# Attention layer: the two halves of a row-maximum block one behind the other, and one VectorE pass over both

## The chip, the core and the metric

The kernel runs on one core of a Trainium2 chip. The metric is device time in microseconds of one launch. Three runs of the kernel before took 2716.44, 2714.80 and 2719.52 us; the median is 2716.44.

## The reference

Two layers over a batch of 8 images of 512 channels and 32x32 places (N = 1024). The first is group norm, attention over the places with 8 heads of 64, a projection and a residual; all in float32:

```
h = group_norm(x, w, b)
q, k, v = split(qkv_w @ h + qkv_b)          # 8 heads of 64 each
attn = softmax(q^T k * 64 ** -0.5)          # 1024 x 1024 for each head
x = x + proj_w @ (v attn^T) + proj_b
```

The second layer picks 256 places of each image, attends among them and projects. The change doesn't touch its arithmetic.

## The kernel before

Float32 products are made of three float32r products of high and low parts (ScalarE makes the high part, VectorE the low one by a subtraction). The first layer is `attention_layer`; each engine has one program written out in order, and semaphores count what is done.

**Steps.** For each of 64 heads (8 images of 8 heads) there are 8 steps, so 512 steps. One step handles one tile t of scores, 1024 columns: two key tiles of 128 for one half (512) of the queries. TensorE in a step (`step`, line 478): the low product of tile t-2 (`weigh_low`, 2 matmuls, line 474), the scores of tile t (4 matmuls of 512 columns, lines 447 and 451) into one of two ring buffers in PSUM, the first half of a row-maximum block (line 428), the projection part that is due in the step, the high product of tile t-1 (`weigh_high`, 4 matmuls), the second half of the block. ScalarE takes two exponentials of the tile (lines 544 and 546): one rounded to float32r, one kept in full. VectorE's `p_low` subtracts them (line 695). The score buffer of tile t-2 and the low product both wait for `p_low` of t-2.

**Row maxima.** Softmax needs the maximum of each query's scores before they are exponentiated. A block is 128 queries against all 1024 keys, taken with high parts alone: two matmuls of 512 columns whose weights are every fourth column of q. There are 8 blocks for a head, one in each step, three steps ahead of their use (`max_tile`). Each half lies in a PSUM bank of its own and is reduced by VectorE on its own (line 679) into `row_max`; after four blocks a small maximum of the two halves (`top_of_halves`, line 687) gives `row_max_top`, and SyncE copies it into a row of `q_low_max` (`max_to_row`).

**Projections.** A unit is 12 matmuls of 512 columns in one PSUM bank: k, q or v of the pair of heads that comes next, or one part of the output (o) of the image before. `PAIR_STEPS` says at which step a unit begins, and whether it is taken whole or in two halves of 6 matmuls in neighbouring steps. "g" is a small matmul for the group norm of the next image, "vt" four 128x128 transposes of v. A finished unit is read by ScalarE (`kq_high`, line 575, `v_full`, `v_high`) and by VectorE (`kq_low`, line 708, `v_low`, `residual`). In the same way VectorE has, at set steps, the statistics of the next image's tiles (`tile_stats`, in the fourth head of an image), the low part of its normed form (`normed_low`, sixth and seventh head) and the low part of the output (`o_low`, first step of every second head). GpSimd multiplies by the reciprocals (line 878).

**Banks.** Scores take two ring buffers of two banks, the weighted sums one bank. Three banks (`BANKS`) serve both units and halves of blocks. `bank_events` lists in order of the program what needs a bank, in units of one matmul, and `assign_banks` gives each the bank that is expected to be read soonest; `READ_BEHIND` says how long behind its last matmul each kind is expected to be read. A first half may not take the bank of a unit that ended in the step before. `fill_free` makes TensorE wait, before the first matmul into a bank, until what was there has been read. VectorE's order in a step (line 799): second half of the block of the step before, the maximum of halves where it is due, `p_low` of the tile before, first half of this step's block, then the low parts of the units that ended in the step before, then statistics and the rest.

Of the kernel before, what the change touches and what calls it, by code (L numbers as in the profile page):

```python
# [14 lines left out]
P = 128  # L15
# [127 lines left out]
READ_BEHIND = dict(m=8, k=26, q=26, v=12, vt=28, o=26, g=22)  # L143


def bank_events():
# [4 lines left out]
    def take(e, closed=None):  # L151
        if e not in last:
            events.append((e, closed))
        last[e] = at
# [4 lines left out]
    for h in range(ALL_HEADS):  # L159
        for s in range(STEPS):  # L160
            block = max_tile(h, s)
            at += 7
            if block:

                take(("m", *block, 0), before(h, s))
# [3 lines left out]
            at += 5  # L169
            if block:  # L170
                take(("m", *block, 1))
# [6 lines left out]
def assign_banks():  # L178
# [3 lines left out]
    for e, closed in events:  # L182
        open_banks = [i for i in range(BANKS) if closed is None or holder[i] not in UNITS.get(closed, [])]
# [29 lines left out]
def attention_layer(nc, x, w_pieces, bias_half, bias_v, bias_o, gn_wb, x1, consts):  # L213
# [23 lines left out]
    sb("spare", [P, 2, N])  # L237
# [5 lines left out]
    mcol = sb("row_max", [P, 2, 2, NT])  # L243
# [14 lines left out]
    ring, pv = tiles[:, 0:2, :], tiles[:, 2, HALF:N]  # L258
    banks = [tiles[:, 2, 0:HALF], tiles[:, 3, 0:HALF], tiles[:, 3, HALF:N]]
# [11 lines left out]
    s_mtop = sem("s_mtop")  # L271
# [36 lines left out]
    def max_bank(h, i, n):  # L308
        return banks[BANK["m", h, i, n]]
# [17 lines left out]
    def tensor(pe, then):  # L327
        mm = nc.tensor.matmul

        def max_count(h, i, n):  # L330
            return (h * NT + i) * 2 + n + 1

        def fill_free(u):
# [3 lines left out]
            if w[0] == "m":  # L337
                pe.wait_ge(s_mx, max_count(*w[1:]))
# [66 lines left out]
        def take_first_max(i, n):  # L405

            if n == 0 and i % 4 == 0:
# [3 lines left out]
            m = i * 2 + n  # L411
            if m > 3:
                pe.wait_ge(s_mx, m - 3)
            first = (i // 4) * HALF + i % 4
            mm(ring[:, i % 2, n * HALF:(n + 1) * HALF], q1[:, 0, first:first + HALF - 3:4],
               k1[:, 0, n * HALF:(n + 1) * HALF], start=True, stop=True).then_inc(s_max, 1)

        def take_max(h, i, n):

            g = h // 2  # L420
            if h % 2 == 0 and i == 0:
                pe.wait_ge(s_kql, kq(("k", g, n)))
# [5 lines left out]
            mm(max_bank(h, i, n)[:, :], q1[:, q_slot(h), first:first + HALF - 3:4], k1[:, k_slot(h), n * HALF:(n + 1) * HALF],  # L428
               start=True, stop=True).then_inc(s_max, 1)

        def scores(h, s):
            t, wk, wq = h * STEPS + s, k_slot(h), q_slot(h)
            if t > 1:
                pe.wait_ge(s_pl, t - 1)
            else:
                pe.wait_ge(s_mx, 2 * (NT - AHEAD))
# [41 lines left out]
        def step(h, s):  # L478
# [5 lines left out]
            if block:  # L484
                take_max(*block, 0)
# [1569 lines left out]
```

## Time and profile before

| what | value |
|---|---|
| median of 3 runs | 2716.44 us |
| span of the one profiled execution | 2718.4 us |
| TensorE matmul | 2619.7 us busy (96%), 11856 matmuls |
| TensorE weight loads | 2181.7 us (80%) |
| VectorE | 2055.1 us (76%) |
| ScalarE | 1578.5 us (58%) |
| GpSimd | 221.9 us (8%) |

The span is the profiled execution's time from its first to its last instruction; no other time of that execution is known. Matmuls overlap, so that a busy TensorE isn't TensorE at its peak: a matmul of 512 columns is shown with some 0.39 us and the next starts 0.23 us after it. The first layer lasts until about 2217 us, the second from there on.

### The profile page before, as it was taken

The numbers are of one execution on the slowest core, as the hardware profiler recorded it, in microseconds if no ns is written. First come the engines' busy times: TensorE is split into PE (matmuls) and PEld (weight loads), VectorE is DVE, ScalarE is ACT, GpSimd is POOL, SyncE is SP. The second block draws the span as 40 slices with busy tenths as digits, with TensorE's granted clock in tenths as the row PEclk, the third lists the DMA queues.
The fourth block names the chain that finished last, engine by engine and source line by source line (L and its number), as shares of the span: only waits on it lengthen the run. The fifth ranks groups of instructions, "written<-read, shape, count | busy, mean of one in ns | idle before, by whom it ended". The sixth has DMA issues, their size and how long they took to land.

```text
span 2718.4 us, 33180 instructions
## 1 busy us (share of the span) xinstructions
PE 2619.7 (96%) x11856; PEld 2181.7 (80%) x11856; DVE 2055.1 (76%) x3294; ACT 1578.5 (58%) x1930; POOL 221.9 (8%) x134
## 2 busy tenths in 40 slices
PE   6999999999999999999999999999999987899998
PEld 5788888888888888888888888888888876688887
DVE  6788768876887688768876887688767867878864
ACT  4667646764676467646764676567646663334311
POOL 1000000000000000000000000000000012111010
PEclk9999999999999999999999999999999999899999
DMA  4512232223222322232223222321322335466444
GB/s 156 177 50 80 67 103 61 79 71 100 64 78 67 101 67 76 63 107 67 65 72 109 66 59 79 109 67 48 90 83 58 112 127 203 171 215 246 165 164 170
DMA packets 154849, 279.48 MB, mean 103 GB/s; under 512 B 51776, under 2 KB 52032, under 8 KB 154176
## 3 DMA queue, kind: packets, MB, share of 16 engines
q1 hardware_dynamic: 152128, 268.98, 31.4%
q0 software_dynamic: 2560, 8.39, 1.0%
q8 instruction: 96, 1.57, 0.2%
q14 instruction: 65, 0.53, 0.1%
HBM read 180.04 MB, written 63.18 MB: 89 GB/s over the span
## 4 chain that ended last, share of the span: by engine, by line
PE 83%; DVE 9%; issue 3%; DMA 2%; ACT 1%; SPq 0%; POOL 0%; POOLq 0%; DVEq 0%; ACTq 0%
PE tiles L372 9%; PE tiles L373 8%; PE tiles L374 8%; PE tiles L474 8%; PE tiles L451 8%; PE tiles L428 8%; PE tiles L468 8%; PE tiles L467 8%; PE tiles L447 7%; PE tiles L1321 5%; PE tiles L1371 2%; DVE row_max L679 2%; DVE p_low L695 2%; DVE h_low L787 1%; PE tiles L383 1%
## 5 line engine op out<-in xcount | busy, mean ns | idle before, releaser
L679 DVE TENSOR_REDUCE row_max<-tiles 128x1 f32<-128x512 f32 x1014 | 694.5, 685 | 443.4 <-PE tiles L428 440.6
L544 ACT ACTIVATE p_high<-tiles 128x1024 fp32r<-128x1024 f32 x512 | 525.5, 1026 | 595.8 <-PE tiles L451 595.1
L695 DVE TENSOR_TENSOR p_low<-tiles,p_high 128x1024 fp32r<-128x1024 f32 x512 | 623.0, 1217 | 7.0 <-ACT tiles L546 6.2
L546 ACT ACTIVATE tiles<-tiles 128x1024 f32<-128x1024 f32 x512 | 523.0, 1021 | 0.0
L467 PE MATMUL tiles<-p_high,v_high 128*128 128x512 f32 x1024 | 406.5, 397 | 2.2 <-ACT num_den L562 1.5
L428 PE MATMUL tiles<-k_high_low,q_high_high 128*128 128x512 f32 x1014 | 404.8, 399 | 0.2 <-DVE row_max L679 0.2
L468 PE MATMUL tiles<-p_high,v_low 128*128 128x512 f32 x1024 | 402.0, 393 | 0.0
L428 PEld LDWEIGHTS tiles<-k_high_low,q_high_high 128*128 128x128 f32 x1014 | 312.5, 308 | 48.6 <-DVE row_max L679 5.7
L474 PE MATMUL tiles<-p_low,v_high 128*128 128x512 f32 x1024 | 325.8, 400 | 14.9 <-DVE p_low L695 14.6
L451 PE MATMUL tiles<-q_low_max,k_high_one 65*128 65x512 f32 x1024 | 325.8, 399 | 1.9 <-DMA q_low_max<-row_max_top 1.8
L372 PE MATMUL tiles<-h_high,w_high 128*128 128x512 f32 x768 | 304.6, 397 | 17.3 <-DVE row_max L679 8.3
L878 POOL TENSOR_TENSOR o_normed<-num_den,o_normed 64x1024 f32<-64x1024 f32 x64 | 153.5, 2399 | 2046.1 <-DMA o_normed<-rec_rows 2046.1
L447 PE MATMUL tiles<-q_high_high,k_high_low 128*128 128x512 f32 x1024 | 316.8, 391 | 0.0
L373 PE MATMUL tiles<-h_low,w_high 128*128 128x512 f32 x768 | 301.7, 393 | 0.0
L374 PE MATMUL tiles<-h_high,w_low 128*128 128x512 f32 x768 | 300.4, 391 | 0.0
L447 PEld LDWEIGHTS tiles<-q_high_high,k_high_low 128*128 128x128 f32 x1024 | 192.0, 188 | 47.6
L451 PEld LDWEIGHTS tiles<-q_low_max,k_high_one 65*128 65x128 f32 x1024 | 193.2, 189 | 45.6 <-DMA q_low_max<-row_max_top 4.4
L474 PEld LDWEIGHTS tiles<-p_low,v_high 128*128 128x128 f32 x1024 | 189.7, 188 | 44.9 <-DVE p_low L695 25.2
L467 PEld LDWEIGHTS tiles<-p_high,v_high 128*128 128x128 f32 x1024 | 192.5, 188 | 38.8 <-ACT num_den L562 2.3
L468 PEld LDWEIGHTS tiles<-p_high,v_low 128*128 128x128 f32 x1024 | 192.6, 188 | 38.0
L372 PEld LDWEIGHTS tiles<-h_high,w_high 128*128 128x128 f32 x768 | 145.8, 190 | 43.9 <-issue 24.2
L374 PEld LDWEIGHTS tiles<-h_high,w_low 128*128 128x128 f32 x768 | 145.1, 189 | 32.4
(167 smaller groups left out, 3138.1 us busy)
## 6 DMA issues: line engine op xcount, KB each, us to landing
x_tiles<-in_x SPq DMA_DIRECT2D x64, 512.0 KB, 5.4
w_high<-w_split SPq DMA_DIRECT2D x126, 256.0 KB, 2.8
w_low<-w_split SPq DMA_DIRECT2D x126, 256.0 KB, 3.0
k_high_one<-k_high_low SPq DMA_DIRECT2D x128, 128.0 KB, 2.3
q_high_high<-q_high_high SPq DMA_DIRECT2D x128, 128.0 KB, 2.3
o_normed<-rec_rows SPq DMA_DIRECT2D x64, 256.0 KB, 3.7
x<-x_tiles SPq DMA_DIRECT2D x32, 512.0 KB, 4.0
x_full<-x SPq DMA_DIRECT2D x32, 512.0 KB, 8.3
```

The source lines that it names most:

```text
L372: mm(fill[:, :], w1, high[:, c, cols], start=(c == 0), stop=False)
L374: last = mm(fill[:, :], w2, high[:, c, cols], start=False, stop=(c == CT - 1))
L428: mm(max_bank(h, i, n)[:, :], q1[:, q_slot(h), first:first + HALF - 3:4], k1[:, k_slot(h), n * HALF:(n + 1) * HALF], start=True, stop=True ...
L447: mm(out[:, n * HALF:(n + 1) * HALF], k1[:, wk, keys[n]], q1[:, wq, queries], start=True, stop=False)
L451: last = mm(out[:, n * HALF:(n + 1) * HALF], k2[0:HD + 1, wk, keys[n]], q2[0:HD + 1, wq, queries], start=False, stop=True)
L467: mm(pv[:, :], weights_of(v1, t, n), p, start=(t % 4 == 0 and n == 0), stop=False)
L468: last = mm(pv[:, :], weights_of(v2, t, n), p, start=False, stop=False)
L474: last = mm(pv[:, :], weights_of(v1, t, n), pl[:, t % 2, n * HALF:(n + 1) * HALF], start=False, stop=(t % 4 == 3 and n == 1))
L544: nc.scalar.activation(ph[:, r, :], ring[:, r, :], ACT.Exp, scale=ATT_SCALE).then_inc(s_ph, 1)
L546: nc.scalar.activation(ring[:, r, :], ring[:, r, :], ACT.Exp, scale=ATT_SCALE).then_inc(s_p32, 1)
L679: nc.vector.reduce_max(mcol[:, h % 2, n, i:i + 1], max_bank(h, i, n)[:, :], AX_X).then_inc(s_mx, 1)
L695: tt(pl[:, r, :], ring[:, r, :], ph[:, r, :].bitcast(F32), ALU.subtract).then_inc(s_pl, 1)
```

## The change

- Both halves of a block are multiplied one behind the other. Where only one unit has a part in the step, they go behind that part; where two have (a unit and a transpose of v), ahead of them (`pair_first`).
- The second half always has the bank in the middle (`MIDDLE`), the first one of the outer banks; units have the outer ones alone. The banks are laid out side by side, so that one VectorE pass of 1024 columns reads both; the weighted sums move to the bank in front of them. A bank is open only when its holder's last matmul is behind.
- One maximum for each block goes straight into `row_max_top`; `row_max`, `top_of_halves` and its semaphore are gone. SyncE's copy waits for the fourth block's maximum.
- VectorE's order in a step: the low parts of the units that ended in the step before, the maximum of this step's block, `p_low` of this step's own tile, then the rest.
- The opening's blocks are handled the same way over the ring buffers.

```diff
-READ_BEHIND = dict(m=8, k=26, q=26, v=12, vt=28, o=26, g=22)
+READ_BEHIND = dict(m=9, k=26, q=26, v=12, vt=28, o=26, g=22)
+MIDDLE = 1
+def pair_first(h, s):
+    spans = (before(h, s), (h, s))
+    begun = {u for at in spans for u, parts in PARTS.get(at, []) if u[0] not in ("g", "vt")}
+    here = {u for u, _ in PARTS.get((h, s), [])}
+    going = {u for u in begun if u in here}
+    return len(going | here) > 1
...
-            at += 7
-            if block:
-                take(("m", *block, 0), before(h, s))
+            at += 6
+            if block and pair_first(h, s):
+                at += 1
+                for n in range(2):
+                    take(("m", *block, n))
             for u, parts in PARTS.get((h, s), []):
                 at += {"g": 1, "vt": 2}.get(u[0], 6 * len(parts))
                 take(u)
-            at += 5
-            if block:
-                take(("m", *block, 1))
+            if block and not pair_first(h, s):
+                at += 1
+                for n in range(2):
+                    take(("m", *block, n), UNITS.get((h, s), []))
+            at += 4
...
-    for e, closed in events:
-        open_banks = [i for i in range(BANKS) if closed is None or holder[i] not in UNITS.get(closed, [])]
+    for e, closed, at in events:
+        among = (MIDDLE,) if e[0] == "m" and e[-1] == 1 else (0, 2)
+        open_banks = [i for i in among if holder[i] not in closed and (holder[i] is None or end[holder[i]] <= at)]
...
-    ring, pv = tiles[:, 0:2, :], tiles[:, 2, HALF:N]
-    banks = [tiles[:, 2, 0:HALF], tiles[:, 3, 0:HALF], tiles[:, 3, HALF:N]]
+    ring, pv = tiles[:, 0:2, :], tiles[:, 2, 0:HALF]
+    pool_row = tiles[:, 2:4, :].rearrange("p a n -> p (a n)")[:, HALF:(1 + BANKS) * HALF]
+    banks = [pool_row[:, i * HALF:(i + 1) * HALF] for i in range(BANKS)]
...
-            fill_free(("m", h, i, n))
+            for n in range(2):
+                fill_free(("m", h, i, n))
...
             scores(h, s)
-            if block:
-                take_max(*block, 0)
+            if block and pair_first(h, s):
+                take_max(*block)
             for u, parts in PARTS.get((h, s), []):
                 unit_work(u, parts)
+            if block and not pair_first(h, s):
+                take_max(*block)
             if t > 0:
                 weigh_high(t - 1)
-            if block:
-                take_max(*block, 1)
...
+        def reduce_max(h, i):
+            if h > 1 and i % 4 == 0:
+                dve.wait_ge(s_mrow[i // 4], 16 * (h - 1))
+            dve.wait_ge(s_max, h * NT + i + 1)
+            first = min(max_banks(h, i))
+            nc.vector.reduce_max(mtop[:, h % 2, i:i + 1], pool_row[:, first * HALF:(first + 2) * HALF], AX_X
+                                 ).then_inc(s_mx, 1)
...
             if t > 0:
-                behind = before(h, s)
-                done = max_tile(*behind)
-                if done:
-                    reduce_max(*done, 1)
-                    if done[1] % 4 == 3:
-                        top_of_halves(done[0], done[1] // 4)
-                p_low(t - 1)
+                for u in UNITS.get(before(h, s), []):
+                    unit_low(u)
             if block:
-                reduce_max(*block, 0)
-            if t > 0:
-                for u in UNITS.get(behind, []):
-                    unit_low(u)
+                reduce_max(*block)
+            p_low(t)
...
         def max_to_row(h, i):
-            sp.wait_ge(s_mtop, 2 * h + i + 1)
+            sp.wait_ge(s_mx, h * NT + 4 * i + 4)
```

## Rows read from the trace of the kernel before

**Rows 1.** The page's chain that ended last, shares of the span by engine.
```profile
PE 83%; DVE 9%; issue 3%; DMA 2%; ACT 1%; SPq 0%; POOL 0%; POOLq 0%; DVEq 0%; ACTq 0%
```

**Rows 2.** Stretches: us; busy (instructions) PE, PEld, DVE, ACT, POOL; PE clock; DMA share; GB/s.
```profile
582.60:856.70 274.10, 271.85 (x1190) 226.13 (x1188) 209.79 (x297) 175.76 (x205) 20.18 (x9) 1.00 0.27 78
2217.00:2718.00 501.00, 453.99 (x2427) 385.18 (x2425) 367.45 (x905) 160.34 (x274) 55.49 (x51) 0.97 0.55 197
46.00:57.00 11.00, 9.02 (x28) 6.67 (x29) 3.13 (x5) 4.25 (x7) 0.00 (x0) 0.69 0.11 39
57.00:110.00 53.00, 49.12 (x212) 39.81 (x211) 43.31 (x62) 36.86 (x49) 0.00 (x0) 1.00 0.65 209
```

**Rows 3.** Groups (busy, mean ns, idle before); then merged time line of the opening.
```profile
L679 DVE TENSOR_REDUCE row_max<-tiles 128x1 f32<-128x512 f32 x1014 | 694.5, 685 | 443.4 <-PE tiles L428 440.6
...
L687 DVE TENSOR_TENSOR row_max_top<-row_max 128x4 fp32r<-128x4 f32 x128 | 37.6, 294 | 4.4
...
37.68 1.01 PEld L415 LDWEIGHTS tiles<-k_high_low,q_high_high 128*128 128x128 f32 x4
...
38.34 3.68 DVE L669 TENSOR_REDUCE row_max<-tiles 128x1 f32<-128x512 f32 x6 [1.17 <-PE tiles L415]
```

**Rows 4.** Time line, one step: start, us, engine, line, operation, output, inputs, count.
```profile
804.60 0.62 PE L447 MATMUL tiles<-q_high_high,k_high_low 128*128 128x512 f32 x2
...
805.14 1.23 DVE L695 TENSOR_TENSOR p_low<-tiles,p_high 128x1024 fp32r<-128x1024 f32 x1
...
806.28 0.68 DVE L679 TENSOR_REDUCE row_max<-tiles 128x1 f32<-128x512 f32 x1
...
806.66 1.02 ACT L546 ACTIVATE tiles<-tiles 128x1024 f32<-128x1024 f32 x1
...
807.60 1.36 ACT L575 ACTIVATE k_high_low<-tiles,bias_qk 64x512 fp32r<-64x512 f32 x2
...
808.05 0.39 PE L428 MATMUL tiles<-k_high_low,q_high_high 128*128 128x512 f32 x1
...
808.48 0.69 DVE L679 TENSOR_REDUCE row_max<-tiles 128x1 f32<-128x512 f32 x1 [0.40 <-PE tiles L428]
```

**Rows 5.** Time line, TensorE: first score matmuls of steps 3.0, 3.1, 4.2-4.4, 6.0-6.2.
```profile
697.31 0.40 PE L447 MATMUL tiles<-q_high_high,k_high_low 128*128 128x512 f32 x1
...
702.65 0.62 PE L447 MATMUL tiles<-q_high_high,k_high_low 128*128 128x512 f32 x2
...
738.16 0.62 PE L447 MATMUL tiles<-q_high_high,k_high_low 128*128 128x512 f32 x2
...
741.29 0.39 PE L447 MATMUL tiles<-q_high_high,k_high_low 128*128 128x512 f32 x1
...
745.80 0.39 PE L447 MATMUL tiles<-q_high_high,k_high_low 128*128 128x512 f32 x1
...
793.11 0.39 PE L447 MATMUL tiles<-q_high_high,k_high_low 128*128 128x512 f32 x1
...
796.99 0.40 PE L447 MATMUL tiles<-q_high_high,k_high_low 128*128 128x512 f32 x1
...
800.46 0.62 PE L447 MATMUL tiles<-q_high_high,k_high_low 128*128 128x512 f32 x2
```

**Rows 6.** Time line about step 2.7: a GpSimd product and the maximum of halves.
```profile
693.14 2.39 POOL L878 TENSOR_TENSOR o_normed<-num_den,o_normed 64x1024 f32<-64x1024 f32 x1 [36.60 <-DMA o_normed<-rec_rows]
...
694.51 1.04 DVE L687 TENSOR_TENSOR row_max_top<-row_max 128x4 fp32r<-128x4 f32 x1
```

**Rows 7.** Time line, VectorE: the low part of one k unit, two heads.
```profile
740.34 1.51 DVE L708 SCALAR_TENSOR_TENSOR k_high_low<-tiles,bias_qk,k_high_low 64x512 fp32r<-64x512 f32 x2
```

**Rows 8.** Time line, end of step 2.7: a residual and the load behind it.
```profile
695.47 1.21 DVE L695 TENSOR_TENSOR p_low<-tiles,p_high 128x1024 fp32r<-128x1024 f32 x1
...
696.74 0.30 PEld L474 LDWEIGHTS tiles<-p_low,v_high 128*128 128x128 f32 x2 [0.51 <-DVE p_low L695]
```

**Rows 9.** Time line, VectorE: statistics of one x tile.
```profile
713.22 1.28 DVE L780 BATCH_NORM_STATS2 bn_parts<-x_tiles 128x6 f32<-128x512 f32 x2
```

More of the change, by code:

```diff
@@ L235, in attention_layer @@
     pl = sb("p_low", [P, 2, N], F32R)
-    sb("spare", [P, 2, N])
+    sb("spare2", [P, 4, HALF])
     nd = sb("num_den", [P, 2, N])
@@ L242, in attention_layer @@
     v32 = sb("v_full", [P, HALF])
-    mcol = sb("row_max", [P, 2, 2, NT])
+    sb("spare", [P, 2, 2, NT])
     mtop = sb("row_max_top", [P, 2, NT], F32R)
@@ L306, in fill_of, with max_banks @@
         return banks[BANK[u]]
-    def max_bank(h, i, n):
-        return banks[BANK["m", h, i, n]]
+    def max_banks(h, i):
+        return [BANK["m", h, i, n] for n in range(2)]
     h32 = Count([(0, 0)] + [(b, t) for b in range(1, BATCH) for t in range(CT)])
@@ L403, in unit_work, with take_first_max @@
                 project(u, parts)
[L405 to L407 removed]
+        def take_first_max(i):
+            if i % 4 == 0:
                 pe.wait_ge(s_kqh, kq(("q", 0, i // 4)))
@@ L425, in take_max @@
                 pe.wait_ge(s_twin["q", i // 4], 32 * (g + 1))
-            fill_free(("m", h, i, n))
+            for n in range(2):
+                fill_free(("m", h, i, n))
             first = (i // 4) * HALF + i % 4
-            mm(max_bank(h, i, n)[:, :], q1[:, q_slot(h), first:first + HALF - 3:4], k1[:, k_slot(h), n * HALF:(n + 1) * HALF],
-               start=True, stop=True).then_inc(s_max, 1)
+            to = max_banks(h, i)
+            for n in range(2):
+                last = mm(banks[to[n]], q1[:, q_slot(h), first:first + HALF - 3:4],
+                          k1[:, k_slot(h), n * HALF:(n + 1) * HALF], start=True, stop=True)
+            last.then_inc(s_max, 1)
         def scores(h, s):
@@ L497, in tensor @@
                 for i in range(4):
-                    for n in range(2):
-                        take_first_max(i, n)
+                    take_first_max(i)
             if u == ("v", 0, 1):
-                for n in range(2):
-                    take_first_max(4, n)
+                take_first_max(4)
         pe.wait_ge(s_pset, 3)
@@ L852, in vector @@
         for i in range(4):
-            for n in range(2):
-                reduce_first_max(i, n)
-        top_of_halves(0, 0)
-        for n in range(2):
-            reduce_first_max(4, n)
+            reduce_first_max(i)
+        reduce_first_max(4)
         for u in PROLOGUE[6:]:
@@ L864, in vector @@
                 step(h, s)
-        p_low(TILES - 1)
         reciprocal(ALL_HEADS - 1)
```

48 lines of the change are left out of this document (18 added, 30 removed).

## The prediction

> **What bounds the kernel now.** I read the chain of waits first: TensorE holds 83% of the chain that ended last, VectorE 9% [rows 1]. The stretch table comes next. It has to be read by stage: one whole batch image of the first layer (a "batch" below) lasts 274.10 us and TensorE is busy 271.85 of them at full clock; the second layer, from about 2217 us, lasts 501 us and is not touched by the change beyond one wait at its start [rows 2]. So in the part that changes TensorE is the bound, there is next to nothing to win on VectorE as such (209.79 busy of 274.10 [rows 2]), and only two things count: the holes in TensorE's stream that go, and those that come. The third view is the time line of one half-unit step, scores to scores 4.15 us [rows 4], and the fourth the starts of steps that last longer than their matmuls need [rows 5].
>
> Holes of one batch now, from [rows 5] (heads 0 to 7, steps 0 to 7, so 3.0 is head 3 step 0): 3.0 lasts 702.65 - 697.31 = 5.34 where 4.15 do: 1.19; 4.3 4.51: 0.36; 4.2 3.13 where 12 matmuls and the small sum need 2.94: 0.19; the same two again at 4.5 and 4.6: 0.55; 6.0 3.88 and 6.1 3.47 where 2.79 do (twelve matmuls): 1.09 and 0.68. Step 2.7 loses 0.3 on average: there the tiny maximum of halves took 1.04 instead of 0.16 us, until GpSimd's product was over (693.14 + 2.39), and the residual pass behind it came late [rows 6]. Together about 4.3 us a batch. The whole of what can be won is six to eight times that, some 30 us, and a few us at the start, where TensorE is idle 1.98 + 3.88 us up to 110 us [rows 2].
>
> **The change part by part.** Matmuls: the same 1014, same strided weights. Two back to back follow each other at the pace of the rest: six maxima of the opening over two ring buffers keep VectorE fed at 0.61 us each (3.68 for six), and their loads, 0.31 long, start 0.23 apart (four in 1.01) [rows 3]. I take 0 (bounds -2 to +4 us in all).
>
> VectorE: a 128x512 maximum has 685 ns, a start-to-start pace of 0.61 [rows 3]; a 128x1024 pass over PSUM 1.23 us, the next one starting 1.14 after it (805.14 to 806.28 [rows 4]). The fused maximum isn't in the trace. Bounds: 0.61 (no dearer than one half) and 1.37 (twice 685 ns). I take 1.13, the row of the same width and memory, a hundredth off for its own variation. So a block costs 1.13 in place of 1.22, and the 128 maxima of halves (294 ns each, 37.6 us [rows 3]) go. In themselves both are worth nothing, TensorE's stream covers them; what they free is the 0.3 at step 2.7. The VectorE page of the Trainium skill ("VectorE: DVE Perf Modes", The perf-mode tier table) says that a reduction runs at single rate from any memory and gives (N+151)/0.96 ns for one fp32 pass: 1.22 us at 1024, 0.69 at 512. By it the lower bound is out; the trace shows this for 512 (685 ns) only.
>
> Order: VectorE did, in a step, second half of the block before, residual of the tile before, first half, low part of a finished projection. Now: low part of the projection that ended a step ago, then the fused maximum, then the residual of this step's own tile. The residual comes earlier for who needs it: it ends 5.3 us after the scores' start and is wanted at about 7.6. Its holes at 6.0/6.1 stay, those at 2.7 and 3.0 shrink. Copying to the row needs no step of its own and SyncE's DMA leaves some 0.9 us sooner; nothing waits for it in the steady state.
>
> Banks: this is where it costs. Three banks, but now the second half of every block has the middle one, so projections and first halves share two. A unit that runs in step t+1 holds one; the pair of step t+1 therefore must take the one whose projection ended in step t, unless that has been read. Following the planner's rule, k and q are handed over like this at 2.3, 2.5, 3.2, 5.0, 5.2, 6.4, 6.6, 7.0, 7.2 with half a unit in front, at 4.2 and 4.5 with only the group sum in front. When is the bank read? Clock the step from its first score matmul (804.60 [rows 4]). Scores end at 0.93, six projection matmuls start from 0.93 to 2.06, the pair at 2.29 and 2.53, v matmuls to 3.67, the low part to 4.15. VectorE starts 0.43 after the last matmul (808.05 to 808.48), so the maximum at 2.96, the residual at 4.09 (its input, the second exponential, ends at 3.08: 806.66 + 1.02), the low part of k or q at 5.22, and that takes 1.51 [rows 7]: 6.73. ScalarE's half of it (807.60, 1.36 long) is ready at 4.4 and not in the way. Into the next step that is 6.73 - 4.15 = 2.58, its weight load can go at 2.64 (0.06 from VectorE's end to the load, 696.68 to 696.74 [rows 8]), and it was due at 2.06 (a load is 0.23 ahead of its matmul): 0.58 late. A load that comes late gives 0.12 back (scores at 697.31 are 0.57 behind the late load where three spacings of 0.23 are usual [rows 5, 8]). Stall 0.46. The next step starts with the same phases, so stalls don't grow or melt.
>
> The list for a batch, by the same phases:
> - eight plain hand-overs (all above but 3.2): 8 x 0.46 = 3.7
> - 3.2: the statistics of an x tile (1.28 for both halves [rows 9], 1.44 with the small aggregate) stand ahead of q's low part in step 3.1; load at 4.08 for 2.06: 1.9
> - 4.2 and 4.5: the pair is due right behind the small sum, load at 0.81, bank free 2.64: 2 x 1.7 = 3.4
> - 3.4 (pair first, then a transpose into its bank): the maximum waits for statistics and reciprocal of step 3.3, ends 3.85, the transposes were due at 2.54: 1.25. The like of it at 0.3, 5.4, 7.4 without statistics: 3 x 0.2 = 0.6
> - 1.1, behind o_low and q's low part: 0.2; 3.0: 0.2; 6.0 and 6.1, where a residual of h stands in each step as before: 0.45 + 0.6 = 1.05
>
> Sum 12.3 against 4.3: +8.0 a batch, six full batches +48. The first batch has the later heads' list (+6.5 over its own holes) and an opening where whole projections wait for a maximum that now goes behind them: I take -5 of the 5.9 us idle there [rows 2] (it can't be more than 5.9, nor above 0), +1.5 net. The last batch has no statistics, sums or h: about 3.1 against 4.7, and 1 less in its last steps: -2.6. Sum +47. The one profiled execution lasts 2718.4, 2.0 over the median 2716.4 of the runs (0.07%, inside their spread), so 2716.4 + 47 = 2763.
>
> What waits behind the new wait: TensorE is in order, so v matmuls of the tile before, the low part and the next scores all stand behind the pair; ScalarE and VectorE then idle, both have room (175.76 and 209.79 of 274.10 [rows 2]). Before, the pair's second half came last in the step, 1.6 us later, and any of three banks could serve.
>
> **Rivals.**
> (a) Faster: the hand-over is met. It decides at the fused maximum's pace: at 0.61 instead of 1.13 (the lower bound) k's low part ends at 6.2, load 2.11 for 2.06, and the eight plain stalls are gone; 3.2 keeps 1.4, 4.2 and 4.5 1.2 each, the rest 0.3, so 4.1 a batch against 4.3, -1 for six; the opening -5, the rest of the first batch -1.4, the last -5.4: 2704. For it: nothing but that the trace has no such pass. Against: both widths cost by the element [rows 3, 4].
> (b) Dearer: the pass takes two halves' full 1.37. Each of some 18 hand-overs is 0.24 later: +4.3 a batch, +31 in all: 2794. For it: it spans two banks. Against: 1.23 for a residual over two banks [rows 4].
> (c) Phases 0.25 sooner than I stack them (they are sums of five small gaps): 12 binding places, -3 a batch and a little in the outer ones, -23: 2740.
> (d) The change doesn't do what it says: the planner finds banks that were read anyway and moves holes about, no net: 2716. Against: two banks for two takers.
>
> **How the numbers follow.** Forecast 0.70, (a) 0.09, (b) 0.09, (c) 0.08, (d) 0.04. Predicted 2763. The range 2728 to 2790 holds the forecast with the small bounds (2750 to 2778, its own range) and (c) and reaches near (b); (a), (d) and part of (b) are left out. Changes under 0.2% (5.4 us) can't be told from none here. Faster by more than that 0.10 ((a) and a little), within it 0.05, slower 0.85.
>
> **What would show it.** Right: the pair's weight loads wait for the low part of k or q, for some 3.7 + 1.9 + 3.4 = 9 us a batch, steps 4.2 and 4.5 last about 4.6 instead of 3.1, 3.2 about 6 instead of 4.15, steps with an output projection stay at 5.51; the fused maximum has about 1.22 us; matmul count unchanged; second layer within 1 us. Wrong: a fused maximum near 0.7 us (then (a)), or steps 2.3, 5.2, 6.4 still at 4.15 with 1.22 (then my phases or my reading of the banks), or new waits on the residual p_low, which I say has more than 0.1 us to spare everywhere, 6.0 and 6.1 the tightest.

## The result: 3.8% slower, and where the 106 us stand

Over four runs each the changed kernel takes 2824.48 us (2815.54 to 2826.21) and the kernel before 2717.98 us: a ratio of 1.0379, 95% interval [1.036, 1.0399]. That is 106.5 us more, outside the range; 46.6 were forecast. The profiled spans are 2718.4 and 2821.7 us, 103.3 apart, and these 103.3 are accounted for below.

The page of the changed kernel first: the chain that ended last, then groups (busy us, mean ns of one | idle before and what ended it).

```profile
PE 70%; DVE 17%; issue 7%; DMA 3%; ACT 2%; SPq 1%; POOL 0%; POOLq 0%; DVEq 0%; ACTq 0%
...
L699 DVE TENSOR_REDUCE row_max_top<-tiles 128x1 fp32r<-128x1024 f32 x507 | 619.8, 1222 | 652.7 <-PE tiles L448 652.1
...
L448 PE MATMUL tiles<-k_high_low,q_high_high 128*128 128x512 f32 x1014 | 349.4, 426 | 57.6 <-DVE k_high_low L720 32.0
L448 PEld LDWEIGHTS tiles<-k_high_low,q_high_high 128*128 128x128 f32 x1014 | 275.6, 313 | 112.4 <-DVE k_high_low L720 46.2
```

VectorE had 9% of the chain [rows 1] and has 17%, although it works less: its one maximum of 1222 ns replaces two of 685 [rows 3]. The pair's weight loads, L448, now stand idle for 112.4 us. The waits of the weight loads say for whom (what waited, for which line; us in all, times, longest):

```profile
PEld tiles L448 <- DVE k_high_low L720: 46.2, 44, 1.7
PEld tiles L448 <- DVE q_low_max L720: 33.7, 38, 2.0
PEld tiles L388 <- issue: 23.5, 19, 6.9
PEld tiles L399 <- DVE row_max_top L699: 19.2, 31, 1.4
...
PEld tiles L472 <- DMA q_low_max<-row_max_top: 13.3, 13, 2.8
```

L720 is the low part of a finished k or q: the bank's last reader. L399 is the transpose of v, which takes the bank of the pair just ahead. L388 is the first matmul of a projection; its "issue" holds a wait that the profile has no releaser for, of which more at step 1.1.

Step by step, from the start of one step's first score matmul to the next one's, for one image; each value is the median over images 1 to 6 (the images are numbered 0 to 7). "More, all" is the sum over the steps named in the row, and "forecast" what the prediction's list comes to for them:

```
steps                                   before       changed      more, all    forecast
2.3 2.5 6.6 | 6.4 (after k)             4.15         4.86 | 5.02   3.00        1.84
5.0 7.0 | 5.2 7.2 (after q)             4.15         4.79 | 4.73   2.44        1.84
3.2                                     4.15         6.11          1.97        1.9
4.2 4.5, and 4.3 4.6 behind them        3.13, 4.51   4.85, 4.17    2.76        2.3
3.4                                     4.61         5.77          1.16        1.25
0.3 5.4 7.4                             4.61         4.8           0.49        0.6
1.1                                     5.51         7.09          1.58        0.2
2.7 3.0                                 3.07, 5.34   2.76, 4.56   -1.09       -1.3
6.0 6.1                                 3.89, 3.46   3.48, 3.40   -0.47       -0.7
other steps with 12 projection matmuls  5.51         5.54          0.37        0
steps with a transpose alone            3.22         3.31          0.36        0
```

The rows sum to 12.6 us an image, against 7.9 forecast. With the steps that moved by a hundredth or two it is 12.9, or 13.1 if each step's difference is taken image by image before the median. The images themselves, 0 to 7, take 14.4, 16.7, 15.4, 14.1, 12.8, 13.1, 12.8 and 0.5 us more; with 1.75 ahead of the first scores and 1.87 behind the last image's they make the 103.3 (the rest is rounding).

How one hand-over looks: TensorE's pair waits in step 2.3 of image 2 (start, us, engine, line, operation). The step begins at 712.39.

```profile
711.20 1.22 DVE L699 TENSOR_REDUCE row_max_top<-tiles 128x1 fp32r<-128x1024 f32 x1 [1.80 <-PE tiles L448]
...
712.34 1.22 DVE L707 TENSOR_TENSOR p_low<-tiles,p_high 128x1024 fp32r<-128x1024 f32 x1
712.39 0.62 PE L468 MATMUL tiles<-q_high_high,k_high_low 128*128 128x512 f32 x2
...
713.59 1.51 DVE L720 SCALAR_TENSOR_TENSOR k_high_low<-tiles,bias_qk,k_high_low 64x512 fp32r<-64x512 f32 x2
...
714.47 0.40 PE L390 MATMUL tiles<-h_high,w_low 128*128 128x512 f32 x1
...
715.15 0.55 PEld L448 LDWEIGHTS tiles<-k_high_low,q_high_high 128*128 128x128 f32 x2 [0.73 <-DVE k_high_low L720]
...
715.62 0.19 PEld L488 LDWEIGHTS tiles<-p_high,v_high 128*128 128x128 f32 x1
```

Maximum, residual and low part follow each other without a gap. The low part ends at 715.10, 2.71 into the step; the pair's load goes at 2.76, where it was due at 2.08, with the last projection matmul (714.47). The order of VectorE's three passes makes the stall: the residual p_low stands between the maximum and the low part that TensorE waits for.

### The profile page after: what moved, and what is told of

Read it like the earlier page. It is cut to its first block, busy times and chain, and to the rows that moved or that the text cites. A ratio compares the mean times of both kernels' runs of the same rounds, so it can differ in the third digit from the quotient of the medians.

```text
span 2821.7 us, 32922 instructions
## 1 busy us (share of the span) xinstructions
PE 2665.3 (94%) x11856; PEld 2188.6 (78%) x11856; DVE 1979.7 (70%) x2654; ACT 1579.2 (56%) x1930; POOL 221.9 (8%) x134
## 4 chain that ended last, share of the span: by engine, by line
PE 70%; DVE 17%; issue 7%; DMA 3%; ACT 2%; SPq 1%; POOL 0%; POOLq 0%; DVEq 0%; ACTq 0%
PE tiles L448 9%; PE tiles L388 7%; PE tiles L390 7%; PE tiles L389 7%; PE tiles L472 6%; PE tiles L489 6%; PE tiles L495 6%; PE tiles L488 6%; PE tiles L468 6%; DVE p_low L707 5%; PE tiles L1323 5%; DVE k_high_low L720 2%; PE tiles L1373 2%; DVE q_low_max L720 2%; DVE row_max_top L699 2%
## 5 line engine op out<-in xcount | busy, mean ns | idle before, releaser
L699 DVE TENSOR_REDUCE row_max_top<-tiles 128x1 fp32r<-128x1024 f32 x507 | 619.8, 1222 | 652.7 <-PE tiles L448 652.1
L448 PE MATMUL tiles<-k_high_low,q_high_high 128*128 128x512 f32 x1014 | 349.4, 426 | 57.6 <-DVE k_high_low L720 32.0
L448 PEld LDWEIGHTS tiles<-k_high_low,q_high_high 128*128 128x128 f32 x1014 | 275.6, 313 | 112.4 <-DVE k_high_low L720 46.2
L495 PE MATMUL tiles<-p_low,v_high 128*128 128x512 f32 x1024 | 319.3, 393 | 1.8 <-DVE p_low L707 1.8
L388 PE MATMUL tiles<-h_high,w_high 128*128 128x512 f32 x768 | 302.6, 394 | 8.7 <-DVE h_low L799 6.8
L472 PEld LDWEIGHTS tiles<-q_low_max,k_high_one 65*128 65x128 f32 x1024 | 192.9, 189 | 53.3 <-DMA q_low_max<-row_max_top 13.3
L388 PEld LDWEIGHTS tiles<-h_high,w_high 128*128 128x128 f32 x768 | 145.5, 189 | 44.5 <-issue 11.4
L389 PEld LDWEIGHTS tiles<-h_low,w_high 128*128 128x128 f32 x768 | 145.7, 190 | 35.4
```

Of the source, the lines that this page charges most:

```text
L388: mm(fill[:, :], w1, high[:, c, cols], start=(c == 0), stop=False)
L389: mm(fill[:, :], w1, low[:, c, cols], start=False, stop=False)
L448: last = mm(banks[to[n]], q1[:, q_slot(h), first:first + HALF - 3:4], k1[:, k_slot(h), n * HALF:(n + 1) * HALF], start=True, stop=True)
L472: last = mm(out[:, n * HALF:(n + 1) * HALF], k2[0:HD + 1, wk, keys[n]], q2[0:HD + 1, wq, queries], start=False, stop=True)
L495: last = mm(pv[:, :], weights_of(v1, t, n), pl[:, t % 2, n * HALF:(n + 1) * HALF], start=False, stop=(t % 4 == 3 and n == 1))
L699: nc.vector.reduce_max(mtop[:, h % 2, i:i + 1], pool_row[:, first * HALF:(first + 2) * HALF], AX_X).then_inc(s_mx, 1)
```

## The experiments

Theory: every microsecond lost is in VectorE's *order*. Projections and first halves share two banks, and a bank's last reader comes late since other passes stand ahead of it; o_low, which the output projection needs, was pushed back in the same way. Main rival: VectorE's *amount* of work, or the fused pass itself. All ratios are against the kernel before, run on the same chip. Steps that another effect touches, a lower clock of TensorE behind a stall, are named where it matters; the section on the prediction comes back to it.

**o_first.** One line moved: o_low from behind p_low to ahead of the maximum.

```
+            if h % 2 == 1 and h > 1 and s == 0:
+                o_low(h // 2 - 1)
             if block:
                 reduce_max(*block)
             p_low(t)
...
-            if h % 2 == 1 and h > 1 and s == 0:
-                o_low(h // 2 - 1)
```

> The changed kernel with one move: o_low (the low part of the finished output pair) goes ahead of the step's fused maximum on VectorE, not behind the residual p_low. Theory A: the 1.58 us that step 1.1 lost (7.09 for 5.54) is TensorE's output projection waiting for o_low, which the change pushed from about 2.9 to about 6.6 us into step 1.0. Then 1.1 returns to 5.54 in seven images, -11 us, about 2813. Rival: it waits for the projection weights, whose transfers were issued at 659.1 and 659.7 in the same step; then nothing moves, 2824.

2812.94 us, 1.0346 [1.0328, 1.0363]; span 2811.7. Step 1.1 went from 7.09 to 5.54 in every image that has it, and no other step's median moved by more than 0.03 but that of 4.2. That one is 4.83 to 4.85 in four of the images 0 to 6 and 6.30, 5.75 and 5.61 in the other three, where the granted clock was 0.73 to 0.85. The changed kernel's rows show the mechanism (step 1.1 of image 2 begins at 658.20):

```profile
658.15 1.22 DVE L707 TENSOR_TENSOR p_low<-tiles,p_high 128x1024 fp32r<-128x1024 f32 x1
...
659.29 1.22 DVE L804 TENSOR_TENSOR o_low<-o_normed,o_high 128x1024 fp32r<-128x1024 f32 x1
...
660.57 0.19 PEld L388 LDWEIGHTS tiles<-o_high,w_high 128*128 128x128 f32 x1 [1.73 <-issue]
```

The first load of the output projection comes 0.06 behind the end of o_low (660.51). In o_first o_low starts at 654.74 and the projection finds it done. The profile names no releaser ("issue") there: an idle stretch without a name is still a wait, and the semaphores in the code say for what.

**low_first.** The low part of a projection right behind the maximum of the step that ends it, ahead of p_low:

```
-            if t > 0:
-                for u in UNITS.get(before(h, s), []):
-                    unit_low(u)
             if block:
                 reduce_max(*block)
+            for u in UNITS.get((h, s), []):
+                unit_low(u)
             p_low(t)
```

> The changed kernel with VectorE's order changed: the low parts of the units that end in step t are taken right behind that step's fused maximum and ahead of its p_low, not a step later. Theory A (loop): a hand-over step is set by the loop pair, maximum 1.14, p_low 1.14, low part 1.51, bank free, pair, 4.8 us against a step of 4.16; taking p_low out of the loop brings 2.3, 2.5, 5.2, 6.6, 7.2 and 5.0, 6.4, 7.0 back to 4.16 (-5.4 an image), 3.2 too (-1.9, the statistics come behind), 4.2 and 4.5 from 4.85 to about 4.05 (-1.6); in return the residual of 2.6 comes late for step 3.0 (+0.8). Net -8 an image, -57 in all, about 2767. Rival B: the stalls come from matmuls and the fused pass meeting in neighbouring banks, whatever the order; then the same steps keep 4.7 to 4.9 and the time 2824 within 5. Rival C: p_low, now a low part later, is the next thing late in every k and q step, 2824 or more.

2775.96 us, 1.0211 [1.0191, 1.0232]; span 2775.3: 46 less than the changed kernel in the spans, where 57 were expected. All nine hand-overs, 2.3 to 7.2, are back at 4.16 us, 3.2 among them; 3.0 too; 4.2 and 4.5 are at 3.86. So the hand-over is the main loss, and it is one of order. It is given back in part at 1.1, where o_low now stands behind still more: 8.6 us instead of 7.09 in images 3 and 6, and 10.2 or more in the other five, where the granted clock was 0.83 and less. The order alone costs 1.5 there and the clock as much again; the expectation had neither. More is given back at 2.7 (3.62) and 6.0 (3.81), where p_low is late for its own reader: 13.8 us of waits for it in place of 3.7.

```profile
PEld tiles L388 <- issue: 31.7, 11, 6.9
PEld tiles L399 <- DVE row_max_top L699: 19.2, 31, 1.4
PEld tiles L495 <- DVE p_low L707: 13.8, 15, 1.4
```

**extras_first.** VectorE's other passes (o_low, statistics of the x tiles but that of 3.4, the small scalings, low parts of the next input and of fresh weights) ahead of the maximum; units and p_low stay.

```
+            if b < BATCH:
+                if h % HEADS == 3 and s in (1, 3, 5):
+                    tile_stats(b, (1, 3, 4, 5).index(s))
...
+            if h % 2 == 1 and h > 1 and s == 0:
+                o_low(h // 2 - 1)
+            if t > 0 and t - 1 + EARLY < len(FRESH):
+                split_low(t - 1 + EARLY)
             if block:
                 reduce_max(*block)
             p_low(t)
```

> The changed kernel with VectorE's occasional work (x statistics of steps 3.1, 3.3 and 3.5, group scale, low parts of h and o, the weight splits of the opening) moved from behind p_low to ahead of the step's fused maximum, where VectorE sits idle 1.7 us. Theory A: 1.1 -1.58, 3.2 from 6.11 to about 4.85 (-1.3), 3.4 from 5.77 to about 4.8 (-1.0), nothing at 6.0 and 6.1, -4 us an image from the second on and a few us in the opening, whose weight splits no longer hold up SyncE's queue: -28 to -35 in all, about 2792. Rival: the maximum comes later by what was put ahead of it, so nothing is won, 2820 to 2830.

2787.76 us, 1.0249 [1.023, 1.0268]; span 2793.6. 1.1 is at 5.54, 3.2 at 4.73, 3.4 at 4.75; the plain hand-overs are untouched, as they should be. What stands ahead of the pair's last reader costs in full, one pass ahead of the maximum nearly nothing.

**halves.** The changed order and banks, but two maxima of 128x512 and the small maximum over four blocks, as before:

```
-            nc.vector.reduce_max(mtop[:, h % 2, i:i + 1], pool_row[:, first * HALF:(first + 2) * HALF], AX_X)
+            nc.vector.reduce_max(mcol[:, h % 2, 0, i:i + 1], banks[to[0]], AX_X)
+            nc.vector.reduce_max(mcol[:, h % 2, 1, i:i + 1], banks[to[1]], AX_X)
+            if i % 4 == 3:
...
+                tt(mtop[:, h % 2, blocks], mcol[:, h % 2, 0, blocks], mcol[:, h % 2, 1, blocks], ALU.max
```

> The changed kernel with the fused pass alone undone: the same banks, order and pairs of matmuls, but two 512-wide maxima back to back and the small maximum of halves after four blocks. Theory A: the pass is worth 0.06 us a step (0.60 + 0.60 against 1.14) plus the small maximum; it binds in some 19 steps an image: +8 to +15 us, 2832 to 2839. Rival B (the pass over two banks is what is slow): 15 us or more faster, below 2810.

2847.77 us, 1.0472 [1.0455, 1.049]. The fused pass by itself is a gain, some 23 us in this kernel, more than the 8 to 15 that were expected of it. It isn't what made the change slow.

**both.** low_first and extras_first together.

> VectorE's order: o_low, the statistics of the x tiles (but that of step 3.4), the small scalings, the low parts of the next image's input and of the fresh weights ahead of the fused maximum; the low part of a projection right behind the maximum of its own step, ahead of the residual p_low. If all that is lost is lost in VectorE's order (my theory), the two gains add: low_first's +7.5 us an image less 4.7 at step 1.1 (10.21 to 5.54, o_low no longer behind anything) less 1.0 at 3.4 gives about +1.9 an image, some +10 in the first image and the opening: about 2738 (2732 to 2746). If the later low part only trades places with the others (rival: VectorE's sum of work in a step is the bound, whatever the order), the extras push the maximum back and it stays at 2765 to 2775.

2736.99 us, 1.0055 [1.004, 1.0071]; span 2734.9. 87 of the 103 us are gone with not one instruction less and the same banks. So VectorE's order made most of the loss, and the rival, that the amount of work binds, falls.

**best.** both, and on TensorE the pair behind the weighing in steps with a group sum, the transpose of v behind it in steps where the pair comes first; on VectorE a unit that ends ahead of an empty step is read in that step.

```
+def behind(h, s):
+    kinds = {u[0] for u, _ in PARTS.get((h, s), [])}
+    return "vt" in kinds if pair_first(h, s) else "g" in kinds
...
             if t > 0:
                 weigh_high(t - 1)
+            for u, parts in behind_it:
+                unit_work(u, parts)
+            if block and not pair_first(h, s) and late:
+                take_max(*block)
```

> As both, and three places moved on top: in steps 4.2 and 4.5 the pair goes behind the weighing with p_high, in steps 0.3, 3.4, 5.4 and 7.4 the transpose of v does, and a unit that ends ahead of a step without a projection has its low part taken in that step, ahead of the maximum. By my theory each of the waits left in low_first goes: 0.7 each at 4.2 and 4.5, 0.14 each at 0.3, 3.4, 5.4, 7.4, 0.86 at 2.7, 0.3 at 6.0: 3.1 us an image or 22 in all, about 2717, no difference from the kernel before. If the banks bind by themselves (rival: two banks for projections and first halves can't be filled without a stall, whatever the order), about 2735 as both.

2725.55 us, 1.0018 [1.0009, 1.0027]; 8 us short of the expectation. 2.7 is back at 2.76 and the transposes' steps at 4.58, but 3.0 pays 0.39 for the first (its scores wait for the copy of the maxima, 1.0 us in image 2), 4.2 and 4.5 gained 0.25 each instead of 0.7 (the residual takes the place of the pair's wait), and 3.6 lost 0.92. The last is plain in VectorE's rows of best: two statistics in a row between two maxima, and in step 3.6 (from 999.38) a transpose that waits for the second maximum.

```profile
997.32 1.28 DVE L807 BATCH_NORM_STATS2 bn_parts<-x_tiles 128x6 f32<-128x512 f32 x2
...
998.95 1.29 DVE L807 BATCH_NORM_STATS2 bn_parts<-x_tiles 128x6 f32<-128x512 f32 x2
...
1000.40 1.17 DVE L714 TENSOR_REDUCE row_max_top<-tiles 128x1 fp32r<-128x1024 f32 x1
```

```profile
1001.62 0.66 PE L406 MATMUL tiles<-identity,v_full 128*128 128x128 f32 x4 [1.16 <-DVE row_max_top L714]
```

**best2.** Each statistic alone behind p_low, where VectorE has no low part of a unit; the low part of a fresh weight between maximum and p_low; low parts of the input in 6.0 and 6.1 behind p_low.

```
+STATS_AT = [(3, 2), (3, 3), (3, 5), (4, 0)]
...
             if block:
                 reduce_max(*block)
+            if t > 0 and t - 1 + EARLY < len(FRESH):
+                split_low(t - 1 + EARLY)
...
             p_low(t)
+            if (h % HEADS, s) in STATS_AT:
+                tile_stats(b, STATS_AT.index((h % HEADS, s)))
```

> The kernel best, where step 3.6 still lost 1.49 us an image (4.71 for 3.22 before) because VectorE made two x tiles' statistics in a row between two maxima (997.3 to 1000.4 of its trace). Here each statistic stands alone behind p_low, in steps 3.2, 3.3, 3.5 and 4.0, in which VectorE has no low part of a projection; the low parts of the next input in 6.0 and 6.1 go behind p_low again; and the low part of a fresh weight goes behind the maximum and ahead of p_low. Theory (TensorE loses only where its bank is read late): 3.6 back to 3.31, 6.0 to 3.5, the first image 1 to 3 us shorter: 1.5 an image, 2712 (2706 to 2718), about 0.3% under the kernel before. Rival (VectorE's work of heads 3 and 4 is too much wherever it stands): the loss moves to 4.1 and 4.2, 2722 to 2727.

2707.25 us, 0.9959 [0.9944, 0.9975]: 0.41% faster than the kernel before and 117 us faster than the changed one. 3.6 is at 3.33 us, 6.1 at 2.76, and the first image is 4.7 us shorter than in best. How much of this is the change's own can't be read from it: some of the moves (the input's low parts in 6.0 and 6.1, where 6.1 took 3.46 in the kernel before; the statistics; the low parts of fresh weights) might serve the kernel before as well, and it was not run with them. Chain and the pair's own row:

```profile
PE 80%; DVE 10%; ACT 4%; issue 3%; DMA 2%; SPq 1%; POOL 0%; DVEq 0%; POOLq 0%; ACTq 0%
...
L457 PE MATMUL tiles<-k_high_low,q_high_high 128*128 128x512 f32 x1014 | 327.4, 404 | 5.9 <-DVE row_max_top L716 5.8
```

The idle time ahead of the pair's matmuls is down from 57.6 to 5.9 us.

**best2_halves.** best2 with the fused pass undone in the same way as in halves.

> best2 with the fused pass undone: two maxima of 128x512 for each pair and the small maximum over four blocks, all else the same. It asks what the one pass over both banks is worth in an order that suits it. Theory: its gain is 0.08 us in each step and the small maximum, and pays only where a bank is waited for; with most of these waits gone it is worth less than the 23 us it was worth in the changed kernel: 2715 to 2722. Rival: VectorE's time is what binds, and it is worth 20 us or more again: 2732 or over.

2726.44 us, 1.0031 [1.0019, 1.0043]: 19.2 us over best2, above the theory's 2715 to 2722 and under the rival's 2732. So the fused pass keeps its value in a good order. The steps that differ are few: 3.0 (+1.02), 2.7 (+0.33), 6.0 (+0.33), 3.4 (+0.13), 4.0 (+0.12). In images 1 and 6, 3.0 lasts 7.1 instead of 5.6, at a lower granted clock: some 3 us of the 20.3 between the two spans are that. In 3.0 of image 2 (from 700.18), for one, a projection's first matmul waits for the second maximum of the pair before it, and VectorE's passes stand back to back:

```profile
697.54 0.80 DVE L726 TENSOR_TENSOR row_max_top<-row_max 128x4 fp32r<-128x4 f32 x1
698.27 1.21 DVE L734 TENSOR_TENSOR p_low<-tiles,p_high 128x1024 fp32r<-128x1024 f32 x1
699.40 1.50 DVE L747 SCALAR_TENSOR_TENSOR q_low_max<-tiles,bias_qk,q_high_high 64x512 fp32r<-64x512 f32 x2
...
701.54 0.68 DVE L722 TENSOR_REDUCE row_max<-tiles 128x1 f32<-128x512 f32 x1
```

```profile
702.37 0.47 PE L398 MATMUL tiles<-h_high,w_high 128*128 128x512 f32 x1 [0.79 <-DVE row_max L722]
```

Here the small maximum, 0.80 instead of 0.16 us, pushes four passes back, as in the kernel before [rows 6]. With it gone they are on time.

**plain_weights.** The changed kernel; the pair's weights are 128 neighbouring columns instead of every fourth. The maxima then belong to other queries, so this is a probe and no kernel to use.

```
-                last = mm(banks[to[n]], q1[:, q_slot(h), first:first + HALF - 3:4],
+                last = mm(banks[to[n]], q1[:, q_slot(h), i * P:(i + 1) * P],
```

> The changed kernel, where the pair takes 128 neighbouring columns of q as its weights in place of every fourth one (the maxima then belong to other queries, so the output is another one); everything else is as it was. If the long weight loads of the pair (0.31 us in place of 0.19) add to a hand-over that stalls (theory), each of the nine hand-overs loses about 0.12 less and steps with an output projection 0.03: 1.5 us an image, about 2812. If loads are hidden even there (rival), the same time within 2 us, 2824.

2804.29 us, 1.0304 [1.029, 1.0318]; span 2810.7. The stalled hand-overs are 0.08 to 0.12 shorter (2.3 at 4.75), the transposes' steps 0.11 to 0.13, those with an output projection 0.04, as the theory has it. It all comes to more than the 12 us expected, since most of the other steps are 0.01 to 0.05 shorter too: the medians of all steps but 4.2, 4.3 and 4.5 sum to 2.7 us less an image, some 19 in seven images, and the two times differ by 20.2. The spans differ by 11.0 only: the profiled execution is the slowest of the five (2812.59), and in it 4.2, 4.3 and 4.5 are 2.5 us an image longer, with a granted clock under 1 in five of the images 1 to 6. The sizes of single steps are what I rest on. The hand-over's rows show the credit:

```profile
712.69 0.30 PEld L448 LDWEIGHTS tiles<-k_high_low,q_high_high 128*128 128x128 f32 x2 [0.75 <-DVE k_high_low L720]
...
713.03 0.19 PEld L488 LDWEIGHTS tiles<-p_high,v_high 128*128 128x128 f32 x1
```

From the late load to the one behind the pair it is 0.34 us, against 0.47 in the changed kernel (715.15 to 715.62).

**split_first.** The changed kernel, with only the low part of a fresh weight ahead of the step's other passes.

```
+            if t > 0 and t - 1 + EARLY < len(FRESH):
+                split_low(t - 1 + EARLY)
             if t > 0:
                 for u in UNITS.get(before(h, s), []):
                     unit_low(u)
```

> The changed kernel, where only the low part of a fresh weight piece (head 0 and 1, steps 0.0 to 1.7 of the first image) goes ahead of the step's maximum and of p_low. Theory: in the opening SyncE's queue stands at the store of that piece, which waits for this low part, and the maxima's copy to the row stands behind it: the opening gets 2 to 4 us shorter, about 2821. Rival: the opening is late because whole projections follow each other and the pair must wait for their low part; then split_low ahead makes that later, and it gets no shorter: 2824 to 2828.

2825.13 us, 1.0375 [1.0353, 1.0397]: no difference in the end, but the start of step 2.1 of the first image comes 3.0 us sooner (124.19 for 127.17), as expected. It was given back in places that the edit doesn't touch: steps 4.2, 4.3 and 4.5 ran at a granted clock of 0.73 to 0.86 in nine places of images 1 to 4, where the changed kernel has five. What it traded is seen in the waits from 47 to 125 us, of the changed kernel:

```profile
PEld tiles L472 <- DMA q_low_max<-row_max_top: 6.2, 3, 2.8
...
PEld tiles L448 <- DVE row_max_top L699: 1.2, 1, 1.2
```

and of split_first:

```profile
PE tiles L448 <- DVE row_max_top L699: 3.0, 2, 2.4
...
PEld tiles L399 <- DVE row_max_top L699: 2.5, 1, 2.5
...
PEld tiles L472 <- DMA q_low_max<-row_max_top: 1.2, 1, 1.2
```

Behind p_low the weight's low part makes the maxima's copy late; ahead of the maximum it holds up the maximum until the weight has come. best2 puts it between the two, and from 47 to 118 us its waits for the copy (1.8) and for the maximum (0.6 at most in one place) are short (17 steps in 69.9 us; 73.8 before, 78.9 changed).

## Why the prediction was wrong

**The direction and the main mechanism held.** The pair's weight loads wait 79.9 us for L720, about 11 an image where 9 were forecast. "Two banks for two takers", nine hand-overs and the two at the group sums, VectorE's low part as the last reader, the fused maximum at 1222 ns (1.13 was taken as its pace; 1.14 measured), 1014 matmuls: all as forecast. Steps 3.2, 3.4, 4.2 to 4.6, 2.7 and 3.0, 6.0 and 6.1 came within 0.5 us of their terms. Rivals (a), (c) and (d), all with a smaller loss or none, are out. (b), a pass as dear as two halves, was to take 31 us more than the forecast, which is 2794 and still 30 short, and its condition doesn't hold: the pass has 1222 ns. halves, which does take both, costs 23 us more than the changed kernel, so that (b)'s price was about right. The formula (N+151)/0.96 ns that the prediction takes from the VectorE page of the Trainium skill ("VectorE: DVE Perf Modes") stands there for a tensor_tensor addition, in the section on the TRN2 errata. That the maximum goes by it was the prediction's own step, and 1222 ns at 1024 columns bears it out.

**Step "1.1, behind o_low and q's low part: 0.2" failed: it is 1.58.** I counted what the *pair* would wait for. But in 1.1 TensorE's first work behind the scores is the output projection, which waits for o_low itself, and VectorE's new order puts that behind maximum and residual. Counted from the start of step 1.0 it had started at 3.5 (not 2.9, as the expectation of o_first has it) and starts at 6.6 now (659.29 - 652.66). The kernel before, whose step 1.0 begins at 619.62:

```profile
623.11 1.21 DVE L792 TENSOR_TENSOR o_low<-o_normed,o_high 128x1024 fp32r<-128x1024 f32 x1
```

o_first gave the whole of it back: 11 us over seven images. I had followed bank readers only and not asked of every pass that was pushed back who reads its output.

**Step "plain hand-over: 0.46" failed: it is 0.58 to 0.71 (0.87 at 6.4).** Two errors of 0.12. "A load that comes late gives 0.12 back" was taken from a load with plain weights [rows 8]; the pair's loads of every fourth column last 0.31 and give nothing back, which plain_weights shows. And behind p_low I let the low part start 1.13 later. So it does for q (46 times, median 1.131) but for k it is 1.247 (54 times): 712.34 to 713.59 above. That is why hand-overs of k lose 0.71 and those of q 0.58. At 6.4 a reciprocal also stands in front of the low part; why 5.0 and 7.0 lose 0.06 more than 5.2 and 7.2 is open. Together 1.8 us an image.

**Small terms that I had at 0.** "The same strided weights, I take 0" for two back to back: steps that carry an output projection or a transpose lost 0.03 to 0.11 each, 0.7 an image; with plain weights that is gone (5.50 and 3.20 us). The bound that I gave for it, +4 us in all, is passed: 7 images by 0.7.

**The opening, "I take -5, +1.5 net" for the first image: it is +14.4.** Step 0.0 did shrink, from 9.27 to 5.18 us. But the first 17 steps together take 78.9 us for 73.8, +5.1 where I had -5, and the rest of the image 9.2 more where I had 6.5. For the opening I left SyncE's queue out. It stores each fresh weight in order when its low part is made, and the copy of the maxima to the row stands behind these stores. In the changed kernel the low part comes last in the step:

```profile
86.69 0.68 DVE L684 TENSOR_TENSOR x_tiles<-x_tiles 128x512 fp32r<-128x512 f32 x1
```

```profile
87.40 0.32 SPq L917 DMA_DIRECT2D w_split<-x_tiles  x1
88.12 0.32 SPq L918 DMA_DIRECT2D w_split<-x_tiles  x1
88.50 0.51 SPq L944 DMA_DIRECT2D q_low_max<-row_max_top  x1
```

```profile
90.89 0.30 PEld L472 LDWEIGHTS tiles<-q_low_max,k_high_one 65*128 65x128 f32 x2 [2.38 <-DMA q_low_max<-row_max_top]
```

The last of the row's maxima had ended at 84.23 (83.00 and 1.23 long), yet its copy left at 88.50, 4.3 us later, and the scores of step 1.0 waited 2.38 for it. Step 1.4 has the same once more:

```profile
112.14 0.50 PEld L472 LDWEIGHTS tiles<-q_low_max,k_high_one 65*128 65x128 f32 x2 [2.77 <-DMA q_low_max<-row_max_top]
```

Behind the two waits the granted clock fell, to 0.82 over step 1.0 and 0.75 over 1.4. split_first shows that both waits go when the low part goes ahead; but it shortens the 17 steps by 1.9 us only, since other waits take their place, so that the rest of the opening's loss is not traced to a cause.

**"Nothing waits for the copy in the steady state" failed too.** I had written that it leaves some 0.9 us sooner. Of the 13.3 us that the changed kernel's weight loads wait for it, 7.0 lie behind the opening, in ten places: some 0.5 at 3.0 in every image (0.15 to 0.49 in five images of the kernel before), 1.18 and 1.48 there in images 1 and 2, and 0.6 to 0.7 at 4.0 in images 2 and 3. In image 2:

```profile
734.87 0.30 PEld L472 LDWEIGHTS tiles<-q_low_max,k_high_one 65*128 65x128 f32 x2 [1.48 <-DMA q_low_max<-row_max_top]
```

**The rest:** the last image, forecast at -2.6, is +0.5, since 1.1 and the plain hand-overs are in it too; 1.75 us ahead of the first scores and 1.87 behind the last image were in no term. Which pass makes the latter was not tried. In numbers, on the spans: six images by 14.15 instead of 8 make 37, the first image 13, the last 3, both ends 3.6: some 56 us between forecast and measurement. Of the 6.15 us by which such an image missed the forecast, the plain hand-overs have 1.8, step 1.1 has 1.4, the small terms 0.7 and the clock, below, 0.8; the rest is spread over the other terms.

**A cost in no term: the clock after a stall.** Images 1 and 2 lost 3.6 and 2.3 us more than the medians' 13.1. At steps 4.2 and 4.3 of image 1 (first two stretches) and 4.5 (third), behind the 1.56 us stalls of the pair at 4.2 and 4.5, the granted clock is below 1; at the same steps 4.2 and 4.3 of image 3 (the last two) it is not. Columns: stretch, us, busy time by engine, PE clock, DMA share, GB/s.

```profile
486.80:492.20 5.40, 3.83 (x15) 3.12 (x14) 4.41 (x6) 2.15 (x3) 0.00 (x0) 0.89 0.21 49
492.20:497.40 5.20, 5.20 (x19) 4.22 (x18) 2.17 (x6) 1.94 (x2) 0.00 (x0) 0.79 0.04 4
501.60:507.90 6.30, 4.73 (x15) 3.82 (x14) 4.94 (x7) 2.72 (x4) 0.00 (x0) 0.74 0.59 167
1066.60:1071.40 4.80, 3.23 (x15) 2.70 (x14) 3.81 (x6) 2.11 (x3) 0.00 (x0) 1.00 0.24 55
1071.40:1075.60 4.20, 4.20 (x20) 3.48 (x19) 2.74 (x7) 1.94 (x2) 0.00 (x0) 1.00 0.03 1
```

4.2, 4.3 and 4.5 last 5.40, 5.19 and 6.34 there, and 4.85, 4.17 and 4.85 at full clock: 3.1 us by the clock alone, with matmuls about 0.43 apart instead of 0.23, the chip's lower level. In image 2 it is 4.2 and 4.3 (clock 0.76 and 0.95), 1.5 us; the remaining 0.6 and 0.9 us of the two images are the longer waits for the copy at 3.0. In images 3 to 6 no step is below full clock. Over all runs, from image 1 on, the steps with a lower clock are 4.2 and 4.5 and those right behind them, 1.1 in low_first, 3.2 and 3.3 in halves and 3.0 in best2_halves: 6 steps in the changed kernel, 5 to 16 in the others that kept long stalls, 2 in best2_halves, and none in before, both, best and best2. So part of what a better order gained is this clock.

## What to carry to other kernels

When a buffer changes hands, list its last reader, and what stands ahead of that reader on its engine: the pass that another engine waits for belongs first, the pass with slack behind it. When passes of an in-order engine are reordered, follow the output of *every* pass that moves back, and every queue that waits for one of them, to its reader, in the opening too. A fused pass can be a gain (19 to 23 us here) inside a change that loses 106; undo the parts one by one before dropping the whole.

## What the runs showed of the hardware

- A weight load of every fourth 4-byte column takes 0.31 us, of neighbouring columns 0.19. With plain weights most steps without a stall were 0.01 to 0.05 shorter, those with a transpose 0.11 to 0.13, the stalled hand-overs 0.08 to 0.12 (plain_weights against the changed kernel).
- A VectorE pass of 64x512 that writes k_high_low starts 1.247 us after a 128x1024 pass, one that writes q_low_max 1.131, at the same width and engine. They differ in the upper partitions written and in reading and writing one tensor; which of the two it is was not tried.
- A maximum of two 128x4 tensors in SBUF takes 0.16 us alone. The 15 of 128 that began during a GpSimd product in the kernel before took 0.35 to 1.92 us, and each ended 0.02 to 0.03 behind the product's end (as in [rows 6], and at 697.54 of best2_halves, where the 16 took 0.80 to 2.12).
- Stalls of 1.5 to 3 us on TensorE were followed in some images by a stretch at 1.2 GHz: in low_first the output projection of step 1.1 of image 2, after a stall of 2.86 us, ran its first eight matmuls 0.43 apart and the rest 0.23; in images 3 and 6 the same stall had no such stretch. A stall can cost more than its length: there some 1.6 us more (10.22 against 8.62 us for the step).
